# A graph network's two convolution passes: a block's running sum as two half chains and a join

## What is computed

```
def gcn_conv(x, edge_index, W, b, num_nodes):
    ...
    h = x @ W
    msg = h[src] * norm[:, None]
    out = jax.ops.segment_sum(msg, dst, num_segments=num_nodes)
    return out + b
h = jax.nn.relu(gcn_conv(x, edge_index, W1, b1, n))
out = jax.nn.relu(gcn_conv(h, edge_index, W2, b2, n))
```

## Time and profile before

| | us |
|---|---|
| median of 3 runs (lowest, highest) | 11233.09 (11230.94, 11240.73) |
| the profiled execution, its span | 11139.42, 11137.6 |
| pass c1: first gather issued, last gather issued | 3790.1, 5956.9 |
| pass c2: first gather issued, last gather issued | 6161.8, 8328.2 |
| pass at: first gather issued, last gather issued | 8643.4, 10908.2 |

### The profile page before, as it was taken

The page is one execution under the profiler, slowest core; times in us unless marked ns, Lnnn a source line. Parts: engine busy times, 40 slices in busy tenths (PEclk is TensorE's granted clock), DMA queues, the critical chain, the costliest instruction groups (busy, mean ns, idle before and its releaser), DMA issues.

```text
span 11137.6 us, 57022 instructions
## 1 busy us (share of the span) xinstructions
PE 1803.2 (16%) x9285; PEld 1517.7 (14%) x9285; DVE 4730.2 (42%) x20005; ACT 1138.0 (10%) x2728; POOL 7065.8 (63%) x6884
## 2 busy tenths in 40 slices
PE   8744444444000400000000000000001000000000
PEld 7733333333000200000000000000000000000000
DVE  8855555555896422222221222222223344444446
ACT  0144444443000100000000000000000000000000
POOL 0566666666103377777776677777767766666665
PEclk7755555555555555555555555555555555555555
DMA  5144444444674111111111111111111222222221
GB/s 225 57 130 131 128 126 131 131 130 114 239 273 166 32 49 46 48 46 46 48 46 38 50 48 46 48 46 46 48 44 27 57 55 56 55 55 56 55 55 43
DMA packets 570444, 911.29 MB, mean 82 GB/s; under 512 B 333436, under 2 KB 348229, under 8 KB 544825
## 3 DMA queue, kind: packets, MB, share of 16 engines
q1 hardware_dynamic: 350264, 652.74, 17.5%
q0 software_dynamic: 219904, 255.88, 10.8%
HBM read 494.12 MB, written 414.02 MB: 82 GB/s over the span
## 4 chain that ended last, share of the span: by engine, by line
issue 44%; DVE 23%; POOL 18%; another core or an unknown queue 12%; PE 3%; DMA 0%; ACT 0%; DVEq 0%; SPq 0%; POOLq 0%; ACTq 0%
POOL arena_a L641 15%; DVE arena_a L1423 6%; DVE arena_b L1112 4%; DVE arena_b L1125 3%; DVE arena_a L1110 3%; POOL arena_a L610 2%; PE bank L811 2%; DVE arena_b L1056 1%; DVE arena_b L1093 1%; DVE arena_a L1599 1%; POOL adst_at_start L624 1%; DVE arena_a L1571 0%; PE bank L916 0%; DVE arena_a L1575 0%
## 5 line engine op out<-in xcount | busy, mean ns | idle before, releaser
L641 POOL DMA_INDIRECT arena_a<-table_c,decay x3136 | 3283.7, 1047 | 1257.9 <-issue 1051.6
L1469 DVE SCALAR_TENSOR_TENSOR arena_a<-arena_a,same_dst 128x64 f32<-128x64 f32 x3134 | 892.1, 285 | 3448.3 <-DVE arena_a L1469 2690.1
L591 POOL DMA_INDIRECT by_src<-arena_b,idx_blk x1568 | 1570.1, 1001 | 825.4 <-issue 449.4
L641 POOL DMA_INDIRECT arena_a<-table_at,decay x1568 | 1521.4, 970 | 744.6 <-issue 468.1
L864 PE MATMUL bank<-ident,chunk_end 128*64 128x128 f32 (+2 forms) x8 | 2.7, 443 | 4428.4 <-DVEq L973 4428.4
L1110 DVE SCALAR_TENSOR_TENSOR arena_a<-arena_a,same_dst 128x64 f32<-128x64 f32 x1567 | 446.0, 285 | 513.3 <-remote 409.7
L864 PEld LDWEIGHTS bank<-ident,chunk_end 128*64 128x64 f32 (+2 forms) x8 | 1.4, 240 | 4429.0 <-DVEq L973 4429.0
L1112 DVE SCALAR_TENSOR_TENSOR arena_b<-arena_a,src_f,before 128x128 bf16<-128x128 f32 x1568 | 546.6, 349 | 15.4 <-issue 14.0
L850 PE MATMUL bank<-hrows 98*128 98x128 f32 x1568 | 404.2, 440 | 626.9 <-DVE arena_b L1125 404.1
L850 PE MATMUL bank<-hrows,arena_a 98*128 98x128 f32 x1568 | 402.9, 438 | 629.1 <-DVE arena_b L1125 390.3
L1215 DVE SCALAR_TENSOR_TENSOR arena_a<-arena_a,mask_blk,hrows 128x96 f32<-128x96 f32 x1567 | 497.1, 317 | 7.4 <-DVE arena_a L1220 4.4
(11 more groups left out here) (279 smaller groups left out, 4808.6 us busy)
## 6 DMA issues: line engine op xcount, KB each, us to landing
arena_a<-ids_rows SPq DMA_DIRECT2D x98, 1024.0 KB
states_src<-arena_a SPq DMA_DIRECT2D x98, 1024.0 KB
states_c<-arena_a SPq DMA_DIRECT2D x196, 512.0 KB
hrows<-by_src SPq DMA_DIRECT2D x98, 776.0 KB, 6.1
states_at<-arena_a SPq DMA_DIRECT2D x98, 576.0 KB
x_at_start<-arena_a SPq DMA_DIRECT2D x7, 7168.0 KB, 49.4
arena_a<-x_at_start SPq DMA_DIRECT2D x98, 512.0 KB
arena_a<-table_c,decay POOLq DMA_INDIRECT x3136
```

Source lines behind the costliest of these rows:

```text
L591: pool.indirect_dma_start(out=by_src, out_offset=AT(ap=idx_blk[r][:, k:k + 1], axis=0), in_=rows[r][:, k, :], in_offset=None)\
L641: pool.indirect_dma_start(out=gb[r][:, k * w:(k + 1) * w], out_offset=None, in_=table[g], in_offset=AT(ap=src_i[:, n * J + k:n * J + k + 1 ...
L1469: ins = v.scalar_tensor_tensor(out=st[h][:, k * D:(k + 1) * D], in0=old, scalar=same_dst[:, e:e + 1], in1=gb[r][:, k * D:(k + 1) * D], op0 ...
```

## The change

The 16 columns of a block are computed in another way, in both convolution passes. Columns 0 to 7 are the chain as before. Columns 8 to 15 are a second chain, from the raw column 8 and without the carried sum, and its steps stand between those of the first: step k of the first and step k of the second, then one increment of `chain` for both. Then eight instructions add to each column of the second half the finished column 7, times the product of the masks in between, `run[8]`. A block so has 8 + 7 + 8 = 23 instructions of DVE instead of 16. It has 9 increments of semaphores instead of 16, and 8 waits on `chain` instead of 15. Bytes, gathers, stores and all other stages are as they were.

```diff
-    ... "chain": (J - 1) * NBLK,
+    ... "chain": J // 2 * NBLK,
...
-                    for k in range(J):
+                    raw = gb[r][:, 0:J * D].rearrange("p (j c) -> p j c", c=D)
+                    made = st[h][:, 0:J * D].rearrange("p (j c) -> p j c", c=D)
+                    carried = chunk_end[:, 0:D] if n == 0 else st[1 - h][:, (J - 1) * D:J * D]
+                    e, half = n * J, J // 2
+                    def join(k, old, scalar, new):
+                        return v.scalar_tensor_tensor(out=made[:, k, :], in0=old, scalar=scalar, in1=new,
+                                                      op0=ALU.mult, op1=ALU.add)
+                    for k in range(half):
                         if k:
-                            old = st[h][:, (k - 1) * D:k * D]
                             v.wait_ge(s("chain"), chained)
-                        elif n == 0:
-                            old = chunk_end[:, 0:D]
-                        else:
-                            old = st[1 - h][:, (J - 1) * D:J * D]
-                        e = n * J + k
-                        ins = v.scalar_tensor_tensor(out=st[h][:, k * D:(k + 1) * D], in0=old,
-                                                     scalar=same_dst[:, e:e + 1],
-                                                     in1=gb[r][:, k * D:(k + 1) * D], op0=ALU.mult, op1=ALU.add)
-                        if k < J - 1:
-                            ins.then_inc(s("chain"), 1)
-                            chained += 1
-                        else:
-                            ins.then_inc(s("state"), 1)
+                        ins = join(k, made[:, k - 1, :] if k else carried, same_dst[:, e + k:e + k + 1], raw[:, k, 0:D])
+                        if k:
+                            old = raw[:, half, 0:D] if k == 1 else made[:, half + k - 1, :]
+                            ins = join(half + k, old, same_dst[:, e + half + k:e + half + k + 1], raw[:, half + k, 0:D])
+                        ins.then_inc(s("chain"), 1)
+                        chained += 1
+                    v.wait_ge(s("chain"), chained)
+                    for k in range(half, J):
+                        ins = join(k, made[:, half - 1, :], run[half][:, n, k - half:k - half + 1],
+                                   made[:, k, :] if k > half else raw[:, half, 0:D])
+                    ins.then_inc(s("state"), 1)
```

More of the change, by code:

```diff
@@ L55 @@
     "table_out": 16 * len(PARTS),
-    "onehots": 2 * NB, "onehots_used": 2 * NB, "flag": 1, "flagrow": 1, "chain": (J - 1) * NBLK,
+    "onehots": 2 * NB, "onehots_used": 2 * NB, "flag": 1, "flagrow": 1, "chain": J // 2 * NBLK,
 }
```

## The result

| | before | after |
|---|---|---|
| median of 5 runs each, side by side (lowest, highest), us | 11233.09 (11229.17, 11240.73) | 11284.37 (11279.56, 11290.68) |
| span of the profiled execution | 11137.6 | 11279.6 |
| c1: first gather to last gather | 2166.8 | 2190.2 |
| c2: first gather to last gather | 2166.4 | 2190.0 |
| c1: last gather to the last step on DVE | 25.2 | 25.2 |

The changed kernel is slower: 1.0044 times the time before, 95% interval 1.0031 to 1.0058, 51 us. The forecast was 11285.

A forecast was written before the change was run, and what follows sets the result against it. Each gather was taken to need 1.40 us of something shared, with one instruction per other engine completing per gather. 10 + 16 = 26 us per pass, 52 for two, on 11233 gave 11285 us, range 11190 to 11430.

The forecast's parts named there:

- The limit is shared, and each instruction takes a place: Passes with gathers: each gather takes 1.40 us of something shared; every other engine may complete one instruction per gather.
- about a dozen gathers on POOL: Gather passes: how far POOL can run ahead of the shared limit, beside a few instructions on DVE.
- POOL's four buffers turn that into stops: c1 and c2: DVE falls behind 9.8 us per block, so POOL stops for it 10 to 30 times per pass.
- (a): c1 and c2: the seven extra instructions' own share, at most 0.027 us each, 0 to 18 us per pass, taken as 10.
- (b): c1 and c2: stop time after the shared thing has emptied, 1.6 us per stop, 0 to 48 per pass, taken as 16.
- The tail stays: End of a pass: DVE's 25 us behind the last gather is bound by the drain; change 0, bounds -15 and 0.
- The offset of 93.7 us: Whole kernel: the median of the runs lies 93.7 us over the profiled execution, carried over to the forecast.
- The second way to the same number: Attention pass against c1: 98 us more for 27 more DVE instructions per block, so 25 us per pass for 7.
- Rival 1: c1 and c2: signals are short, not instructions; POOL keeps 1.25 us, 450 us less, 10783 us; whole or part, chance 0.17.
- Rival 2: c1 and c2: the extra seven instructions are free, each pass stays 1568 x 1.40, 11233 us; chance 0.12.
- Rivals 3 and 4: 3: as attention pass, +196, top of own case (0.66). 4: instructions cost half a gather, +960; 0.05 shared with Rival 5.
- Rival 5: c1 and c2: DVE's operands lock POOL out, 2.0 us per block, +391, 11624 us; chance 0.05 together with rival 4.

The follow-up runs named there:

- the 512-element add of the join: Changed kernel with its last eight instructions per block replaced by one wide multiply and one wide add: 10172.38 us beside 10110.97 for the kernel before.
- the kernel with ten instructions: Kernel before with 10 DVE instructions per block instead of 16, eight of them wide: 10228.92 us beside 10107.4, and 10228.27 in one run.
- the last experiment: Kernel before plus 80 activations, 60 matmuls and 16 tiny stores per block, each store with 16 increments: 10107.84 us in one run, beside 10112.65.
- attempt to bring the limit on by rate: Kernel before plus 80 activations and 60 matmuls per block, 10114.94 us beside 10110.97; then with 16 tiny stores per block too, 10107.84 beside 10112.65.

## Why the prediction was right

**The limit is shared, and each instruction takes a place.** Held, in the profile of after: pairs 2.80 us apart though one of the two signals nobody, 7.5 us behind the eight of the join, and POOL's stops. It is read from traces alone. The reading "about a dozen gathers on POOL" was low: 220 us at 1.25 us are 176 gathers, at 1.40 us 157, so some 19 were ahead.

**POOL's four buffers turn that into stops; gathers go at 1.25 us between them.** Held in kind: stops of POOL, and 947 ns per gather between them. The number was forecast as 10 to 30 with the attention pass's 8.8 us as a guide. There are 45 of 5.3 us on average. The sum (a) + (b) of 26 us per pass came out at 23.4 and 23.6 all the same; how it splits between the instructions' own share and lost time in stops can't be read off. But the 16 us taken for (b) are as much as ten stops that lose 1.6 us each, and 45 stops within 23.4 us can have lost 0.52 us each at most. The number of stops was too low and the loss of one too high, and that the two cancel is luck: 45 stops of 1.6 us would have been 72 us per pass.

**The tail stays.** The number held, 25.2 us before and after; the reason did not. The prediction has the tail bound by the drain and not by DVE's own work. Before, DVE is slow to its last step. In after the last gather is issued at 6034.81 and the slow stretch ends 9.6 us later: from 6044.39 on DVE goes at full speed and needs 15.6 us more for the rest of a block and two whole ones, 5.6 us each, by which it had fallen behind. A shorter drain and work left over add up to the old tail, and nothing shows that they had to.

```profile
6034.81 0.95 POOL L641 DMA_INDIRECT arena_a<-table_c,decay  x1 [0.30 <-issue]
...
6040.94 0.80 DVE L1467 SCALAR_TENSOR_TENSOR arena_a<-arena_a,same_dst 128x64 f32<-128x64 f32 x3 [9.56 <-issue]
...
6044.39 2.55 DVE L1467 SCALAR_TENSOR_TENSOR arena_a<-arena_a,same_dst 128x64 f32<-128x64 f32 x10 [0.92 <-DVE arena_a L1467]
6046.97 1.66 DVE L1467 SCALAR_TENSOR_TENSOR arena_a<-arena_a,hi_src 128x64 f32<-128x64 f32 x8
6048.72 3.90 DVE L1467 SCALAR_TENSOR_TENSOR arena_a<-arena_a,same_dst 128x64 f32<-128x64 f32 x15
```

**The offset of 93.7 us.** Right to carry over. It lay in stages that the change doesn't touch: the profile of after has 54.5 us more ahead of c1 and 37 more in the attention pass.

**The second way to the same number agreed for a reason that doesn't stand.** It read the attention pass's 98 us over c1 as the price of 27 more instructions. Where nothing is short the attention pass takes 2051.9 us and c1 1959.9, also 92 more, without a stop. The gathers of the attention pass are busy for 1575.3 us there, those of c1 for 1483. Some 52 of these 92 us are in the 97 gathers that begin while the pass's own wide operation, L1599, runs; the rest is mostly in gathers beside its other DVE operations:

```profile
9414.72 1.22 DVE L1599 TENSOR_TENSOR arena_a<-arena_a 128x1024 f32<-128x1024 f32 x1
9415.04 1.72 POOL L641 DMA_INDIRECT arena_a<-table_at,decay  x1 [0.30 <-issue]
```

So the bound of 0.027 us per instruction in (a) rested on a difference that has this in it too. That it came close to the truth for the changed kernel is not shown to be more than luck.

**Rival 1 (signals)** fell by the pairs, the stops and 72 gathers per 100 us. Its pace of 1.25 us is real, as the other chips show, but the fewer signals of the change did not bring it. **Rival 2** fell by the 23 us per pass. **Rivals 3 and 4** would have been +98 and +480 per pass. **Rival 5** fell by its price: seven more steps cost 2.0 us per block by it, and 0 to 0.11 where nothing else is short. But the reading "nothing is locked" was wrong.

Taken gather by gather, the traces show a hold, and its size. A gather that begins while a wide operation with two inputs runs on DVE takes longer than its 0.94 us by the rest of that operation less 0.13 us. So it is in the 192 gathers that begin while the 512-element add of the join runs (0.69 us; 0.11 to 0.40 us longer, 0.29 on average) and in the 97 that begin during L1599 with 1024 elements (1.22 us; 0.25 to 0.91 longer, 0.54 on average), each time with a spread of 0.002 us. A gather already under way when such an operation begins is not held: 194 of them in the same run are less than 0.001 us longer on average. What a wide operation costs thus hangs on where the next gather happens to begin, and 13 us per pass, scaled from the number of operations, was no way to forecast it. Steps of 64 elements (0.28 us) leave little: gathers beside them stand 7 to 30 ns further apart on average. The trace of before has it too. There 185 gathers of c1 and c2 begin 0.12 to 0.16 us before the end of a step and take 20 ns more on average; the two that the earlier trace rows show at 0.94 us do not begin there.

The Trainium skill's rule of the lock (SBUF — State Buffer, two separate sides), by which the one that comes second waits for the whole instruction of the first, thus agrees with these gathers where DVE's operation is first. In the other direction no run shows it: all 250 wide operations that begin beside a running gather in that run take 0.69 us. Nor do the runs show that it takes two inputs, since no gather began during the wide copy of the kernel with ten instructions.

**What is behind the 1.40 us stays open.** In the first two profiles the limit and the loss of recorded increments stand together in the passes with gathers, and both are away in "src". It isn't a slower engine: a step of DVE takes 285 ns in the first profile and in the later one. The Trainium skill (NOTIFIC — the notification-queue block, 7.1, Overflow) says that the block that writes the records can hold back an engine, and the counts above agree with it. That is a coincidence in place, not a proof: in time the loss comes first and the slower gathers some 200 us later, and in the last experiment some records are missing at full pace. No execution without records was had, neither attempt to bring the limit on by rate succeeded, and whether it hangs on the chip or on something else of the first sitting isn't known. What was meant to part instructions from signals by experiment could not be tried where the limit is; that rests on the pairs of after alone.

No version beats the kernel before: without the limit all are bound by POOL's 1.25 us per gather, and with it the seven further instructions per block cost 51 us.

## What to carry to other kernels

A shorter dependent chain on an engine that nobody waits for is worth nothing, and the instructions that it is bought with aren't free: they took 51 us where something shared was short. Where engines that have nothing to do with each other fall into the same pace, look for what they share before looking at either, and ask on a second chip whether the pace belongs to the program at all. A number that two ways give alike is only confirmed if the second way doesn't hide a cost of its own; here DVE's hold on POOL, half of it by one wide operation, made up most of the difference.

## What the runs showed of the hardware

- The same program took 11233 us in the first sitting and 10107 to 10116 in the later ones, on five chips, at nearly the same granted clock (0.516, and 0.517 to 0.518). Per pass of 1568 gathers: 2167 and 1960 us.
- A gather of 128 rows is issued in 0.94 us and followed 0.30 us later by the next, 1.25 us in all, and as much beside a thousand small instructions of PE and ACT per 100 us.
- DVE steps that depend on each other and wait for a signal stand 0.32 us apart; eight that don't depend on each other are issued in 1.66 us, 0.2 apart.
- Two-input operations on DVE hold gathers on POOL: 27 us per pass for two of 512 elements per block, 57 for eight. Only gathers that begin while such an operation runs are held, each for the rest of the operation less 0.13 us (spread 0.002 us, operations of 0.69 and 1.22 us); a gather already under way is not.
- 686 more instructions of 64 elements per pass cost nothing in the form of the changed kernel, and 11 us in the form in which both inputs are the same gathered column. Why these differ was not tested; with narrow steps too the hold goes by where in a step a gather begins.
